# Scan phase: the step size by one softplus activation, both halves in succession

## The chip, the cores and the metric

The kernel runs on one core of one Trainium2 chip. The metric is the device time of one execution in microseconds (us), lower is better. Engines: TensorE (PE), VectorE (DVE), ScalarE (ACT), GpSimd (POOL), and SyncE (SP), which issues most of the DMAs. Each works through its own instructions in the order in which they were written, and waits where an instruction needs a semaphore.

## The reference

Sixteen sequences of 512 tokens with 256 channels pass through a selective scan (the mixer) and then, pairwise independent, through two layers of windowed attention and feed-forward (the stack). Only the mixer matters here. For each sequence:

```python
xz = einsum('bld,ed->ble', h, W_in); x_ssm, z = split(xz, 2)      # 512 inner channels each
A = -exp(A_log)                                                   # 512 x 16 states
B_mat, C_mat = x_ssm @ W_B.T, x_ssm @ W_C.T                       # 16 states each
dt = softplus(x_ssm @ W_dt.T + b_dt)                              # the step size, 512 channels
# for each token: h = exp(min(dt * A, 20)) * h + dt * B * x;  y = sum over states of h * C
y = (y + x_ssm * D) * silu(z)
x = x + ga * (y @ W_out.T * sigmoid(output_gate))
```

## The kernel before

`mixer_pass` handles one sequence in about 109 us. Channels lie on the 128 partitions, tokens along the free axis. The 512 inner channels are four chunks `d`; two chunks are a half. The scan is cut into 32 units `q` of 128 channels x 2 states x 512 tokens: units 0 to 15 belong to the first half, 16 to 31 to the second. For one unit

- ScalarE computes the decays, `exp(dt * A)`, two activations (step `decay`, line 701), into one of three SBUF slots or, for ten units, into PSUM;
- TensorE spreads the rows of B over the partitions (step `bcast`, line 576) and VectorE multiplies them by `u = dt * x` in PSUM (step `mul`, line 762). For the ten units 2, 3, 8, 9, 12, 13, 18, 19, 24, 25 a DMA spreads B and GpSimd multiplies (line 832), so these have no `bcast`;
- VectorE scans (step `scan`, line 779);
- GpSimd multiplies by C (step `cmul`, line 839);
- TensorE adds the unit to the sum over states (step `sum`, line 584), after which its state slot, one of six, is free.

A `bcast` of unit q waits for scan q-2, since the two PSUM slots take turns. The gates (`gate`, line 785) need the last sums of their half: gate 2 that of unit 30, gate 3 that of unit 31.

Beside the units of sequence s-1, in the same pass, the products of sequence s are made in two PSUM banks called `work`, one bank for each product, in turn: `xs`, `bc`, `z` (lines 540 to 551). `dt` (`project_dt`, line 553) is the exception: one half takes both banks at once, twelve matmuls, and it has to wait until both have been read. `softplus` (line 670) then turns a half into the step size. Before, this is done in parts on three engines: ScalarE writes `relu(v)`, `exp(-|v|)`, a mask, a square for a series, and `ln(1 + exp(-|v|))`; VectorE (step `step`, `step_size`, line 748) evaluates the series and puts it where the mask says; GpSimd (step `dtadd`, `add_parts`, line 811) adds the two parts (line 815), then makes `u` (line 818) and sets the marks in `dt` that separate the two states of a unit (line 822). The bank release of `dt` hangs on VectorE's `log_chosen`.

The order of all steps is one list written out by hand, `MIXER_ORDER` (line 140). Each engine takes its own steps from it in that order. The list holds three sequences at once: "-" after a step's name moves it one sequence back. Written with ~ for sequence s-1, the stretch around the change reads, engine by engine:

```
TensorE: sum14~ sum15~ dt0 bcast20~ skip1~ bcast21~ sum16~ sum17~ bcast22~ sum18~ bcast23~ sum19~ sum20~ sum21~
         z0 z1 z2 bcast26~ z3 bcast27~ sum22~ dt1 bcast28~ sum23~ bcast29~ sum24~ sum25~ bcast30~ bcast31~
         sum26~ sum27~ sum28~ bcast0 bcast1 sum29~ sum30~ sum31~ skip0 out0~
ScalarE: decay18~ bcmid0 xscopy3 decay19~ decay20~ decay21~ decay22~ soft0 decay23~ decay24~ zcopy0 decay25~
         zcopy1 zcopy2 decay26~ decay27~ zcopy3 decay28~ decay29~ soft1 decay30~ decay31~ decay0 decay1
VectorE: scan17~ gate0~ bclow0 gate1~ scan18~ scan19~ mul20~ mul21~ scan20~ scan21~ mul22~ mul23~ scan22~ step0
         scan23~ scan24~ scan25~ mul26~ mul27~ scan26~ scan27~ mul28~ mul29~ scan28~ scan29~ mul30~ mul31~
         scan30~ scan31~ mul0 mul1 step1 gate2~ scan0 gate3~ scan1 scan2 scan3
GpSimd:  cmul16~ to cmul21~ mul24~ mul25~ cmul22~ cmul23~ cmul24~ dtadd0 cmul25~ to cmul31~ mul2 mul3 cmul0
         cmul1 dtadd1 cmul2
```

In the first pass there is no sequence before, and only the steps without ~ run: they follow one another with nothing beside them. ScalarE's functions come in table sets; a change of set is an instruction of its own (ACT_TABLE_LOAD). In a pass there are two changes, to silu and back to exp and ln (lines 649 and 650).

Of the kernel before, what the change touches and what calls it, by code (L numbers as in the profile page):

```python
# [22 lines left out]
P = 128  # L23
BATCH, SEQ, DIM = 16, 512, 256
# [3 lines left out]
INNER_CHUNKS = D_INNER // P  # L28
# [6 lines left out]
SERIES_ROOT = 3.0 ** 0.5  # L35
# [11 lines left out]
SERIES_BELOW = 0.02  # L47
# [4 lines left out]
EXP_AND_LN = "natural_log_exp_and_others"  # L52
MOD_SHIFT_A, MOD_SCALE_A, MOD_GATE_A, MOD_SHIFT_B, MOD_SCALE_B, MOD_GATE_B = range(6)
# [48 lines left out]
def host_constants():  # L102
# [32 lines left out]
    1: "xload xT xcopy stat norm hT mod up hcut xs xscopy bc bccopy cstore bcup bcrest bcmid bclow dt soft step dtadd"  # L135
# [8 lines left out]
scan-:15 mul-:16 cload:6 scan-:16 bload:9 mul-:17 bcast-:13 bcrest-:0 decay-:22 cmul-:15 mul-:18 soft-:0 scan-:17  # L144
decay-:23 bcast-:14 bcast-:15 mul-:19 cload:7 cload:8 gate-:0 bclow-:0 gate-:1 cmul-:16 cmul-:17 decay-:24 zcopy-:0
cmul-:18 cmul-:19 cmul-:20 decay-:25 sum-:10 zcopy-:1 cstore:0 sum-:11 bc-:0 bcast-:16 scan-:18 zcopy-:2 decay-:26
decay-:27 cload:9 sum-:12 zcopy-:3 decay-:28 bload:12 scan-:19 bcast-:17 cload:10 decay-:29 cmul-:21 sum-:13 mul-:20
mul-:21 soft-:1 scan-:20 xs-:3 sum-:14 bcast-:18 scan-:21 decay-:30 mul-:22 mul-:23 sum-:15 mul-:24 mul-:25 dt-:0
cmul-:22 decay-:31 scan-:22 bcast-:19 bcast-:20 decay:0 step-:0 skip-:1 scan-:23 decay:1 stat:0 cload:11 bcast-:21
# [3 lines left out]
h2store:0 sum-:22 dt-:1 cmul-:30 bcast-:28 scan-:29 sum-:23 bcast-:29 mul-:30 sum-:24 mul-:31 sum-:25 xcopy:0 decay:6  # L153
bcast-:30 scan-:30 bcast-:31 sq2:0 sum-:26 sum-:27 scan-:31 bload+:1 mul:0 sum-:28 decay:7 mul:1 bcast:0 bcast:1
sum-:29 step-:1 dev2:0 cmul-:31 decay:8 bcast:2 gate-:2 scan:0 mul:2 gate-:3 scan:1 xcopy:1 scan:2 scan:3 decay:9
mul:3 mul:4 res:0 sum-:30 mod:0 cmul:0 scan:4 sum-:31 skip:0 decay:10 out:0 bcast:3 res:1 cmul:1 bcast:4 mul:5 out:1
dtadd-:1 sum:0 bcast:5 up:0 cmul:2 scan:5 xT:0 bcast:6 mod:1 cen2:0 decay:11 up:1 cmul:3 cmul:4 mean2:0 decay:12 mul:6
sum:1 cmul:5 mul:7 scan:6 bcast:7 mul:8 scan:7 xn2:0 decay:13 bload+:4 scan:8 xscopy:0 sum:2 decay:14 decay:15
decay:16 xscopy:1 h2:0 scan:9 mul:9 xscopy:2 bcast:8 cmul:6 var2:0 bccopy:0 mul:10 xT:1 hcut:0 mul:11 cmul:7 cmul:8
sum:3 cmul:9 sum:4 hcut:1 scan:10 scan:11 bcast:9 hT:0 decay:17 bcup:0 hT:1  # L160
# [61 lines left out]
def mixer_pass(nc, inp, mod, x1_dram, stack_dram, bc_dram):  # L222


    with ExitStack() as ctx:
        def sb(name, shape, dt=F32):
            return ctx.enter_context(nc.sbuf_tensor("a_" + name, shape, dt))
# [12 lines left out]
        work = ctx.enter_context(nc.psum_tensor("a_work", [P, 2, SEQ], F32))  # L240
# [8 lines left out]
        skip_mat = sb("skip_mat", [P, INNER_CHUNKS, P])  # L249
# [6 lines left out]
        b_dt = sb("b_dt", [P, INNER_CHUNKS])  # L256
        skip_d = sb("skip_d", [P, INNER_CHUNKS])
        ln_eps = sb("ln_eps", [P, 1])
        root, above = sb("root", [P, 1]), sb("above", [P, 1])
        half_cut = sb("half_cut", [P, 2, 1])  # L260
        waiter = sb("waiter", [P, 2])
        xt = sb("xt", [P, TILES, DIM])
        xn = sb("xn", [P, TILES, DIM])
        neg_mean = sb("neg_mean", [P, TILES])
# [43 lines left out]
        abs_done = signal("abs_done", INNER_CHUNKS)  # L308
        exp_done = signal("exp_done", 2)
        series_begun = signal("series_begun", 2)  # L310
        series_done = signal("series_done", 2)
        log_chosen = signal("log_chosen", 2)
        dt_sum = signal("dt_sum", 2)
# [16 lines left out]
        x1_done = signal("x1_done", CHUNKS)  # L330
# [55 lines left out]
        def first_statistics(act):  # L386
# [4 lines left out]
                      root, above, half_cut, skip_mat, signals, sems_cleared, (neg_mean, token_rate), load_first_x, first_statistics)  # L391
# [8 lines left out]
        sp_p = sb("sp_p", [P, 2, SEQ])  # L400
        sp_ln = sb("sp_ln", [P, 2, SEQ])
        sp_mask = sb("sp_mask", [P, 2, SEQ])
# [17 lines left out]
                    "dt": (log_chosen, 1), "out": (x1_done, 1), "mean2": (xc2_done, 1), "var2": (xn2_done, 1)}  # L420
# [187 lines left out]
        def _(act):  # L608
# [61 lines left out]
            def softplus(s, slot, half):  # L670


                wait(act, x1_done, s - 2, CHUNKS)
                for dd in range(2):
                    d = 2 * half + dd
                    wait(act, dt_full, s, d + 1)
                    nc.scalar.activation(dt[slot][:, d, :], work[:, dd, :], ACT.Relu, bias=b_dt[:, d:d + 1])
                    nc.scalar.activation(work[:, dd, :], work[:, dd, :], ACT.Abs, bias=b_dt[:, d:d + 1]).then_inc(abs_done.sem, 1)
                wait(act, abs_done, s, 2 * half + 2)
                nc.scalar.activation(work[:], work[:], ACT.Exp, scale=-1.0).then_inc(exp_done.sem, 1)  # L680
                wait(act, exp_done, s, half + 1)
# [45 lines left out]
        def _(dve):  # L727
# [20 lines left out]
            def step_size(s, slot, half):  # L748

                wait(dve, series_begun, s, half + 1)  # L750
                nc.vector.scalar_tensor_tensor(work[:], sp_p[:], 13.0 / 16, work[:], ALU.add, ALU.mult).then_inc(series_done.sem, 1)
                wait(dve, series_done, s, half + 1)
                nc.vector.memset(waiter[:, half:half + 1], 0.0)
                nc.vector.copy_predicated(sp_ln[:], sp_mask[:].bitcast(I32), work[:]).then_inc(log_chosen.sem, 1)

# [50 lines left out]
            pipeline(dve, {"hcut": cut_h, "bcrest": rest_of_bc, "bclow": lower_bc, "step": step_size, "mul": scan_input, "scan": scan,  # L806
                           "gate": gate, "res": residual, "cen2": centre_tail, "xn2": normalise_tail})

        @block.gpsimd
        def _(pool):  # L810
            def add_parts(s, slot, half):

                pair = slice(2 * half, 2 * half + 2)
                wait(pool, log_chosen, s, half + 1)
                nc.gpsimd.tensor_tensor(dt[slot][:, pair, :], dt[slot][:, pair, :], sp_ln[:], ALU.add).then_inc(dt_sum.sem, 1)
                wait(pool, dt_sum, s, half + 1)
                wait(pool, xs_done, s, INNER_CHUNKS)
                nc.gpsimd.tensor_tensor(u[slot][:, pair, :], dt[slot][:, pair, :], xs[slot][:, pair, :], ALU.mult)\
                    .then_inc(u_done.sem, 1)
                wait(pool, u_done, s, half + 1)  # L820

                nc.gpsimd.tensor_tensor(dt[slot][:, pair, 0:1], half_cut[:], half_cut[:], ALU.add).then_inc(dt_done.sem, 1)

            def scan_input(s, slot, q):
                if q not in by_pool:
                    return
                j, d, dd = unit(q)
                k = q // 2
                wait(pool, u_done, s, d // 2 + 1)
# [12 lines left out]


# [1020 lines left out]
def setup_weights(nc, inp, banks, ident, mean_mat, pick, picks, w_in_t, w_dt_in, w_bc_in, w_out_t, neg_a, b_dt, skip_d, mod, ln_eps,  # L1864
                  root, above, half_cut, skip_mat, signals, cleared, to_zero, load_first_x, first_statistics):


    with ExitStack() as ctx:
# [42 lines left out]
        with nc.Block() as block:  # L1911
# [68 lines left out]
            def _(dve):  # L1980
# [3 lines left out]
                nc.vector.memset(root[:], -SERIES_ROOT / 4)  # L1984
                nc.vector.memset(above[:], SERIES_BELOW)
# [80 lines left out]
```

## Time and profile before

| | |
|---|---|
| runs | median 4442.51 us of 3 (4442.38 to 4449.84) |
| span of the profiled execution | 4447.4 us |
| busy: TensorE | 4082.2 us (92%) |
| busy: VectorE | 3664.9 us (82%) |
| busy: ScalarE | 2681.4 us (60%) |
| busy: GpSimd | 2692.2 us (61%) |
| VectorE, tenths in 40 slices | `4999999999999999667778787777878777787874` |
| GpSimd, tenths in 40 slices | `2999999999999999553433333343433334433332` |
| granted TensorE clock, tenths | `8999999999999999869999999999999999999998` |

The profile is one execution on the chip. The span is cut into 40 slices of 111 us each; a digit is the busy share in tenths, 9 is 90% or more. The mixer is about the first 41% of the span (to 1850 us), the stack is the rest. In a timeline, a row starts with the start of the instruction and its length, and ends with "xN" where N like instructions in a row are merged; in brackets stands how long the engine was idle before it, and what ended that. Instructions of one engine overlap a little, so the cost of one in a full row is the distance to the next start.

### The profile page before, as it was taken

To read this page: it belongs to the slowest core of one execution; us is meant where nothing else is said; L and a number is where in the kernel's file an instruction comes from. 1 tells how busy PE (TensorE), PEld (TensorE's weight loads), DVE (VectorE), ACT (ScalarE), POOL (GpSimd) and SP (SyncE) were. 2 spreads that over 40 slices of the span, in tenths; PEclk is the share of its full clock that TensorE was granted. 3 is DMA by queue.
4 is the path that set the end of the run, shared out by engine and by line. 5 is a ranking of instruction groups with operands and counts; after the bars stand their busy time and mean duration, and the time that the engine had idled before them with its cause. 6 is when DMAs were issued, how large, how long until landed. Compare 5 with 4: busy or idle time off the path is not lost. (4 is left out here: it accounts for less than half of the span.)

```text
span 4447.4 us, 60346 instructions
## 1 busy us (share of the span) xinstructions
PE 4082.2 (92%) x19614; PEld 2634.6 (59%) x19614; DVE 3664.9 (82%) x6079; ACT 2681.4 (60%) x5831; POOL 2692.2 (61%) x1329
## 2 busy tenths in 40 slices
PE   6999999999999998659999999999999999999997
PEld 4444444444444444347777777776767777677775
DVE  4999999999999999667778787777778787777874
ACT  5677777777777776335656555555646555565654
POOL 2999999999999999553433333343433334343332
PEclk8999999999999999869999999999999999999998
DMA  2333333333333333420000000001020100101000
GB/s 84 107 117 114 115 114 119 115 115 119 119 114 114 115 119 111 141 77 29 15 29 15 29 15 29 15 19 58 20 78 20 34 25 25 34 20 39 20 29 24
DMA packets 118502, 295.05 MB, mean 66 GB/s; under 512 B 21208, under 2 KB 43664, under 8 KB 118192
## 3 DMA queue, kind: packets, MB, share of 16 engines
q1 hardware_dynamic: 114544, 290.37, 19.7%
q8 instruction: 160, 2.62, 0.3%
q10 hardware_dynamic: 3648, 0.83, 0.1%
q14 instruction: 150, 1.23, 0.1%
HBM read 248.52 MB, written 42.64 MB: 65 GB/s over the span
## 5 line engine op out<-in xcount | busy, mean ns | idle before, releaser
L839 POOL TENSOR_TENSOR a_state<-a_state,a_c_wide 128x1024 f32<-128x1024 f32 x512 | 1196.8, 2377 | 32.4 <-DVE a_state L779 31.4
L584 PE MATMUL a_y_sum<-a_state,a_ident 128*128 128x512 f32 x2048 | 948.2, 600 | 2.4 <-POOL a_state L839 2.4
L1667 POOL TENSOR_TENSOR b_scores<-b_scores,b_row_rate 128x1024 f32<-128x1024 f32 (+1 forms) x256 | 426.6, 1682 | 731.0 <-DVE b_row_rate L1782 731.0
L779 DVE TENSOR_TENSOR_SCAN a_state<-a_decay,a_slot 128x1024 f32<-128x1024 f32 x352 | 790.7, 2272 | 3.4 <-issue 0.4
L1640 POOL TENSOR_TENSOR b_by_cos<-b_qk,b_rotary 128x1024 f32<-128x1024 f32 x128 | 309.0, 2414 | 604.3 <-DVE b_qk L1717 604.3
L1340 PE MATMUL b_bank<-b_w_qkv,b_hx_part 128*128 128x512 f32 x2304 | 628.7, 413 | 41.0 <-DVE b_qk L1717 18.3
L584 PEld LDWEIGHTS a_y_sum<-a_state,a_ident 128*128 128x128 f32 x2048 | 388.2, 192 | 407.8 <-issue 343.2
L1545 ACT ACTIVATE b_scores<-b_scores,b_row_bias 128x256 f32<-128x256 f32 (+1 forms) x1024 | 478.0, 471 | 204.8 <-DVE b_row_bias L1771 203.2
L701 ACT ACTIVATE a_decay<-a_dt,a_neg_a 128x512 f32<-128x512 f32 x704 | 458.8, 712 | 107.5 <-DVE a_state L779 105.3
L1340 PEld LDWEIGHTS b_bank<-b_w_qkv,b_hx_part 128*128 128x128 f32 x2304 | 421.3, 193 | 161.0 <-issue 44.0
L1451 PE MATMUL b_bank<-b_hn_part,b_w 128*128 128x512 f32 x2112 | 508.5, 398 | 7.3 <-DVE b_hn_part L1689 7.1
L1451 PEld LDWEIGHTS b_bank<-b_hn_part,b_w 128*128 128x128 f32 x2112 | 396.0, 189 | 103.2 <-DVE b_hn_part L1689 9.6
L762 DVE TENSOR_TENSOR a_slot<-a_u,a_slot 128x1024 f32<-128x1024 f32 x352 | 417.7, 1214 | 23.9 <-PE a_slot L576 23.2
L832 POOL TENSOR_TENSOR a_state<-a_u,a_b_wide 128x1024 f32<-128x1024 f32 x160 | 376.0, 2375 | 4.5 <-PE a_y_sum L584 4.1
L701 ACT ACTIVATE a_slot<-a_dt,a_neg_a 128x512 f32<-128x512 f32 x320 | 208.1, 683 | 280.9 <-DVE a_state L779 280.1
L779 DVE TENSOR_TENSOR_SCAN a_state<-a_slot,a_state 128x1024 f32<-128x1024 f32 x160 | 356.7, 2269 | 2.1 <-ACT a_slot L701 1.2
L1674 POOL TENSOR_TENSOR b_h_part<-b_h,b_h_part 128x512 fp32r<-128x512 f32 x160 | 206.4, 1290 | 248.8 <-ACT b_h_part L1606 248.8
L1765 DVE CUSTOM_DVE_ANT_0 b_scores<-b_bank,b_squares 128x256 f32<-128x256 f32 (+1 forms) x1024 | 338.1, 386 | 0.3 <-issue 0.3
L1837 DVE SCALAR_TENSOR_TENSOR b_h<-b_bank,b_b_1a,b_gelu 128x512 f32<-128x512 f32 x192 | 143.6, 749 | 188.0 <-POOL b_h_part L1674 116.7
L1500 ACT ACTIVATE b_qk_rot<-b_bank 128x512 f32<-128x512 f32 x256 | 142.7, 597 | 242.2 <-PE b_bank L1340 241.4
L1472 PE MATMUL b_bank<-b_h_part,b_w 128*128 128x512 f32 x1088 | 285.9, 401 | 0.0
L576 PE MATMUL a_slot<-a_bc_parts,a_picks 96*128 96x512 bf16 x704 | 212.1, 384 | 80.0 <-DVE a_state L779 79.5
(210 smaller groups left out, 7042.4 us busy)
## 6 DMA issues: line engine op xcount, KB each, us to landing
a_c_wide<-bc_rows SPq DMA_DIRECT2D x256, 512.0 KB, 3.7
a_b_wide<-bc_rows SPq DMA_DIRECT2D x80, 512.0 KB, 4.8
b_hx<-stack_rows SPq DMA_DIRECT2D x64, 256.0 KB, 3.8
b_x_res<-stack_rows SPq DMA_DIRECT2D x32, 512.0 KB, 4.0
a_xt<-in_L_attn_x SPq DMA_DIRECT2D x16, 512.0 KB, 6.1
x_rows<-a_x_t SPq DMA_DIRECT2D x16, 512.0 KB, 5.4
stack_rows<-a_h_t SPq DMA_DIRECT2D x16, 512.0 KB, 5.4
stack_rows<-b_xc SPq DMA_DIRECT2D x16, 512.0 KB, 2.9
```

Source lines behind the costliest of these rows:

```text
L584: last = nc.tensor.matmul(y_sum[dd][:], ident[:], state[state_ring.slot[q]][:, i, :], start=False, stop=(j == GROUPS - 1 and i == GROUP - 1))
L701: last = nc.scalar.activation(to[:, i, :], dt[slot][:, d, :], ACT.Exp, scale=neg_a[:, d, n:n + 1])
L762: nc.vector.tensor_tensor(slots[q % 2][:], u[slot][:, d, :].unsqueeze(1).to_broadcast([P, GROUP, SEQ]), slots[q % 2][:], ALU.mult).then_in ...
L779: nc.vector.tensor_tensor_scan(flat(h), flat(factor), flat(term), 0.0, ALU.mult, ALU.add).then_inc(scan_done.sem, 1)
L832: nc.gpsimd.tensor_tensor(state[state_ring.slot[q]][:], u[slot][:, d, :].unsqueeze(1).to_broadcast([P, GROUP, SEQ]), b_wide[b_ring.slot[k] ...
L839: nc.gpsimd.tensor_tensor(h[:], h[:], c_wide[c_ring.slot[q // 2]][:], ALU.mult).then_inc(cmul_done.sem, 1)
L1340: last = nc.tensor.matmul(psum.tile(name)[:], x[:, c, w * P:(w + 1) * P].bitcast(F32R), weights[:, c, cols:cols + INNER].bitcast(F32R), st ...
L1451: last = nc.tensor.matmul(psum.tile(f"{stem}{m}")[:], weights[:, c, at * P:(at + 1) * P].bitcast(F32R), x[:, c, :].bitcast(F32R), start=(n ...
L1545: e = nc.scalar.activation(scores[w % 2][:, h, lo:hi], scores[w % 2][:, h, lo:hi], ACT.Exp, bias=row_bias[:, w, h:h + 1], accum_out=row_su ...
L1640: nc.gpsimd.tensor_tensor(by_head(by_cos), by_head(qk), for_heads(rotary[:, w, 0], DIM_HEAD), ALU.mult)\
L1667: nc.gpsimd.tensor_tensor(probs, probs, row_rate[:, w, at].unsqueeze(2).to_broadcast([P, 4, hi - lo]), ALU.mult)\
L1765: last = nc.vector.tensor_tensor_reduce(out=scores[w % 2][:, head, lo:hi], in0=psum.tile(f"s{w}_{g}_{h}")[:, at + lo:at + hi], in1=mask[:, ...
```

## The change

The step size becomes one activation `Softplus` with the bias, written directly to `dt`, for each of the four chunks. The relu, abs, exp, mask, square and ln activations go, as do VectorE's `step` and GpSimd's first add. A change of table set to `softplus` stands ahead of half 0, and one back to exp and ln behind half 1. In the order, `soft1` moves right behind `soft0` on ScalarE (from behind decay29~ to ahead of decay23~), and `dt1` right behind `dt0` on TensorE (from behind sum22~ to ahead of bcast20~). Both banks of `dt` are now released by ScalarE's `soft_done`. All other steps keep their order.

```diff
@@ softplus @@
                 wait(act, x1_done, s - 2, CHUNKS)
+                if half == 0:
+                    nc.scalar.preload_act_table_set(SOFTPLUS)
                 for dd in range(2):
                     d = 2 * half + dd
                     wait(act, dt_full, s, d + 1)
-                    nc.scalar.activation(dt[slot][:, d, :], work[:, dd, :], ACT.Relu, bias=b_dt[:, d:d + 1])
-                    nc.scalar.activation(work[:, dd, :], work[:, dd, :], ACT.Abs, bias=b_dt[:, d:d + 1]).then_inc(abs_done.sem, 1)
-                wait(act, abs_done, s, 2 * half + 2)
-                nc.scalar.activation(work[:], work[:], ACT.Exp, scale=-1.0).then_inc(exp_done.sem, 1)
-                wait(act, exp_done, s, half + 1)
-                wait(act, log_chosen, s if half else s - 1, half if half else 2)
-                nc.scalar.activation(sp_mask[:], work[:], ACT.Relu, scale=-1.0, bias=above[:])
-                nc.scalar.activation(sp_p[:], work[:], ACT.Square, scale=1.0 / SERIES_ROOT, bias=root[:])
-                wait(act, dt_sum, s if half else s - 1, half if half else 2)
-                nc.scalar.activation(sp_ln[:], work[:], ACT.Ln, bias=1.0).then_inc(series_begun.sem, 1)
+                    last = nc.scalar.activation(dt[slot][:, d, :], work[:, dd, :], ACT.Softplus, bias=b_dt[:, d:d + 1])
+                last.then_inc(soft_done.sem, 1)
+                if half == 1:
+                    nc.scalar.preload_act_table_set(EXP_AND_LN)
@@ release of the banks @@
-                    "dt": (log_chosen, 1), "out": (x1_done, 1), "mean2": (xc2_done, 1), "var2": (xn2_done, 1)}
+                    "dt": (soft_done, 1), "out": (x1_done, 1), "mean2": (xc2_done, 1), "var2": (xn2_done, 1)}
@@ VectorE @@
-            def step_size(s, slot, half):
-
-                wait(dve, series_begun, s, half + 1)
-                nc.vector.scalar_tensor_tensor(work[:], sp_p[:], 13.0 / 16, work[:], ALU.add, ALU.mult).then_inc(series_done.sem, 1)
-                wait(dve, series_done, s, half + 1)
-                nc.vector.memset(waiter[:, half:half + 1], 0.0)
-                nc.vector.copy_predicated(sp_ln[:], sp_mask[:].bitcast(I32), work[:]).then_inc(log_chosen.sem, 1)
@@ GpSimd, add_parts @@
-                wait(pool, log_chosen, s, half + 1)
-                nc.gpsimd.tensor_tensor(dt[slot][:, pair, :], dt[slot][:, pair, :], sp_ln[:], ALU.add).then_inc(dt_sum.sem, 1)
-                wait(pool, dt_sum, s, half + 1)
+                wait(pool, soft_done, s, half + 1)
                 wait(pool, xs_done, s, INNER_CHUNKS)
```

## Rows read from the trace of the kernel before

**Rows 1.** Busy time by stretches: stretch, us, then each engine, PEclk, DMA share, GB/s.
```profile
1382.19:1491.03 108.84, 100.82 (x299) 48.74 (x298) 108.33 (x72) 78.39 (x134) 107.55 (x49) 1.00 0.35 117
```

**Rows 2.** Timeline of VectorE: start us, us, what, [idle before and releaser].
```profile
1354.11 2.33 DVE L762 TENSOR_TENSOR a_slot<-a_u,a_slot 128x1024 f32<-128x1024 f32 x2
1356.35 4.46 DVE L779 TENSOR_TENSOR_SCAN a_state<-a_decay,a_slot 128x1024 f32<-128x1024 f32 x2
...
1365.17 1.20 DVE L751 SCALAR_TENSOR_TENSOR a_work<-a_sp_p,a_work 128x1024 f32<-128x1024 f32 x1
...
1367.63 2.27 DVE L779 TENSOR_TENSOR_SCAN a_state<-a_decay,a_slot 128x1024 f32<-128x1024 f32 x1
...
1374.18 2.33 DVE L762 TENSOR_TENSOR a_slot<-a_u,a_slot 128x1024 f32<-128x1024 f32 x2
...
1382.19 1.23 DVE L762 TENSOR_TENSOR a_slot<-a_u,a_slot 128x1024 f32<-128x1024 f32 x1 [0.19 <-PE a_slot L576]
...
1396.56 1.23 DVE L751 SCALAR_TENSOR_TENSOR a_work<-a_sp_p,a_work 128x1024 f32<-128x1024 f32 x1
...
1399.07 0.68 DVE L785 TENSOR_TENSOR a_u<-a_y_sum,a_sz 128x512 f32<-128x512 f32 x1
```

**Rows 3.** Timeline of TensorE's matmuls in the same sequence.
```profile
1349.24 3.00 PE L535 MATMUL a_work<-a_h_part,a_w_dt_in 128*128 128x512 f32 x12 [0.70 <-DVE a_bc_parts L745]
1352.16 0.59 PE L576 MATMUL a_slot<-a_bc_parts,a_picks 96*128 96x512 bf16 x2
...
1354.34 0.59 PE L576 MATMUL a_slot<-a_bc_parts,a_picks 96*128 96x512 bf16 x2
...
1367.80 4.40 PE L535 MATMUL a_work<-a_h_part,a_w_in_t 128*128 128x512 f32 x18 [1.10 <-DVE a_sp_ln L754]
...
1381.49 0.60 PE L576 MATMUL a_slot<-a_bc_parts,a_picks 96*128 96x512 bf16 x2
...
1394.55 0.59 PE L576 MATMUL a_slot<-a_bc_parts,a_picks 96*128 96x512 bf16 x2 [0.44 <-DVE a_state L779]
1394.98 5.31 PE L584 MATMUL a_y_sum<-a_state,a_ident 128*128 128x512 f32 x12
```

**Rows 4.** Timeline of ScalarE in the same sequence.
```profile
1349.13 3.78 ACT L701 ACTIVATE a_decay<-a_dt,a_neg_a 128x512 f32<-128x512 f32 x6
1352.81 0.67 ACT L677 ACTIVATE a_dt<-a_work,a_b_dt 128x512 f32<-128x512 f32 x1
1353.38 0.64 ACT L678 ACTIVATE a_work<-a_work,a_b_dt 128x512 f32<-128x512 f32 x1
...
1407.39 1.28 ACT L649 ACT_TABLE_LOAD   x1
1408.68 1.91 ACT L649 ACTIVATE a_sz<-a_sz 128x2048 f32<-128x2048 f32 x1
```

**Rows 5.** Timeline of GpSimd in the same sequence.
```profile
1375.51 2.41 POOL L815 TENSOR_TENSOR a_dt<-a_dt,a_sp_ln 128x1024 f32<-128x1024 f32 x1
1377.99 2.39 POOL L818 TENSOR_TENSOR a_u<-a_dt,a_xs 128x1024 f32<-128x1024 f32 x1
```

**Rows 6.** Timelines of TensorE and ScalarE in the first sequence.
```profile
57.66 3.00 PE L535 MATMUL a_work<-a_h_part,a_w_dt_in 128*128 128x512 f32 x12 [2.62 <-DVE a_bc_parts L745]
68.69 7.99 PE L535 MATMUL a_work<-a_h_part,a_w_in_t 128*128 128x512 f32 x24 [8.02 <-DVE a_sp_ln L754]
...
80.30 1.04 PE L576 MATMUL a_slot<-a_bc_parts,a_picks 96*128 96x512 bf16 x4
...
85.72 2.56 ACT L701 ACTIVATE a_decay<-a_dt,a_neg_a 128x512 f32<-128x512 f32 x4
```

**Rows 7.** Clock: a stretch at half clock, VectorE's stall, TensorE after idle time.
```profile
950.60:954.00 3.40, 3.40 (x6) 1.69 (x5) 3.40 (x3) 1.11 (x2) 3.40 (x2) 0.50 0.49 154
...
958.40 2.36 DVE L762 TENSOR_TENSOR a_slot<-a_u,a_slot 128x1024 f32<-128x1024 f32 x2 [1.42 <-PE a_slot L576]
...
1788.80 0.59 PE L576 MATMUL a_slot<-a_bc_parts,a_picks 96*128 96x512 bf16 x2 [3.43 <-DVE a_state L779]
```

More of the change, by code:

```diff
@@ L34 @@
 POOL_LOADS = (1, 4, 6, 9, 12)
-SERIES_ROOT = 3.0 ** 0.5
 DEPTH, HEADS, DIM_HEAD, WINDOW = 2, 8, 64, 128
@@ L46 @@
 LN_EPS = 1e-5
-SERIES_BELOW = 0.02
 CUT_OFF = 1.2e20
@@ L52 @@
 EXP_AND_LN = "natural_log_exp_and_others"
+SOFTPLUS = "softplus"
 MOD_SHIFT_A, MOD_SCALE_A, MOD_GATE_A, MOD_SHIFT_B, MOD_SCALE_B, MOD_GATE_B = range(6)
@@ L134 @@
 MIXER_STEPS = {
-    1: "xload xT xcopy stat norm hT mod up hcut xs xscopy bc bccopy cstore bcup bcrest bcmid bclow dt soft step dtadd"
+    1: "xload xT xcopy stat norm hT mod up hcut xs xscopy bc bccopy cstore bcup bcrest bcmid bclow dt soft dtadd"
        " z zcopy silu",
@@ L143 @@
 cmul-:14 xscopy-:3 cload:4 decay-:19 cload:5 bcast-:12 sum-:9 decay-:20 xs-:1 xs-:2 decay-:21 mul-:15 scan-:14
[L144 to L149, printed above, removed]
+scan-:15 mul-:16 cload:6 scan-:16 bload:9 mul-:17 bcast-:13 bcrest-:0 decay-:22 cmul-:15 mul-:18 soft-:0 soft-:1
+scan-:17 decay-:23 bcast-:14 bcast-:15 mul-:19 cload:7 cload:8 gate-:0 bclow-:0 gate-:1 cmul-:16 cmul-:17 decay-:24
+zcopy-:0 cmul-:18 cmul-:19 cmul-:20 decay-:25 sum-:10 zcopy-:1 cstore:0 sum-:11 bc-:0 bcast-:16 scan-:18 zcopy-:2
+decay-:26 decay-:27 cload:9 sum-:12 zcopy-:3 decay-:28 bload:12 scan-:19 bcast-:17 cload:10 decay-:29 cmul-:21 sum-:13
+mul-:20 mul-:21 scan-:20 xs-:3 sum-:14 bcast-:18 scan-:21 decay-:30 mul-:22 mul-:23 sum-:15 mul-:24 mul-:25 dt-:0
+dt-:1 cmul-:22 decay-:31 scan-:22 bcast-:19 bcast-:20 decay:0 skip-:1 scan-:23 decay:1 stat:0 cload:11 bcast-:21
 scan-:24 sum-:16 sum-:17 cmul-:23 bcast-:22 sum-:18 bcast-:23 decay:2 sum-:19 scan-:25 decay:3 cmul-:24 sum-:20
@@ L152 @@
 cload:12 bcast-:25 z-:2 mul-:29 bcast-:26 z-:3 scan-:28 cmul-:25 cmul-:26 cmul-:27 norm:0 cmul-:28 cmul-:29 bcast-:27
-h2store:0 sum-:22 dt-:1 cmul-:30 bcast-:28 scan-:29 sum-:23 bcast-:29 mul-:30 sum-:24 mul-:31 sum-:25 xcopy:0 decay:6
+h2store:0 sum-:22 cmul-:30 bcast-:28 scan-:29 sum-:23 bcast-:29 mul-:30 sum-:24 mul-:31 sum-:25 xcopy:0 decay:6
 bcast-:30 scan-:30 bcast-:31 sq2:0 sum-:26 sum-:27 scan-:31 bload+:1 mul:0 sum-:28 decay:7 mul:1 bcast:0 bcast:1
[L155 to L160, printed above, removed]
+sum-:29 dev2:0 cmul-:31 decay:8 bcast:2 gate-:2 scan:0 mul:2 gate-:3 scan:1 xcopy:1 scan:2 scan:3 decay:9 mul:3 mul:4
+res:0 sum-:30 mod:0 cmul:0 scan:4 sum-:31 skip:0 decay:10 out:0 bcast:3 res:1 cmul:1 bcast:4 mul:5 out:1 dtadd-:1
+sum:0 bcast:5 up:0 cmul:2 scan:5 xT:0 bcast:6 mod:1 cen2:0 decay:11 up:1 cmul:3 cmul:4 mean2:0 decay:12 mul:6 sum:1
+cmul:5 mul:7 scan:6 bcast:7 mul:8 scan:7 xn2:0 decay:13 bload+:4 scan:8 xscopy:0 sum:2 decay:14 decay:15 decay:16
+xscopy:1 h2:0 scan:9 mul:9 xscopy:2 bcast:8 cmul:6 var2:0 bccopy:0 mul:10 xT:1 hcut:0 mul:11 cmul:7 cmul:8 sum:3
+cmul:9 sum:4 hcut:1 scan:10 scan:11 bcast:9 hT:0 decay:17 bcup:0 hT:1
 """
@@ L258, in mixer_pass @@
         ln_eps = sb("ln_eps", [P, 1])
-        root, above = sb("root", [P, 1]), sb("above", [P, 1])
         half_cut = sb("half_cut", [P, 2, 1])
-        waiter = sb("waiter", [P, 2])
         xt = sb("xt", [P, TILES, DIM])
@@ L307, in mixer_pass @@
         dt_full = signal("dt_full", INNER_CHUNKS)
[L308 to L313, printed above, removed]
+        soft_done = signal("soft_done", 2)
         u_done = signal("u_done", 2)
@@ L390, in mixer_pass @@
         setup_weights(nc, inp, banks_all, ident, mean_mat, pick, picks, w_in_t, w_dt_in, w_bc_in, w_out_t, neg_a, b_dt, skip_d, mod, ln_eps,
-                      root, above, half_cut, skip_mat, signals, sems_cleared, (neg_mean, token_rate), load_first_x, first_statistics)
+                      half_cut, skip_mat, signals, sems_cleared, (neg_mean, token_rate), load_first_x, first_statistics)
         x_t = [sb(f"x_t{i}", [P, CHUNKS, SEQ]) for i in range(2)]
@@ L399, in mixer_pass @@
         u = [sb(f"u{i}", [P, INNER_CHUNKS, SEQ]) for i in range(2)]
-        sp_p = sb("sp_p", [P, 2, SEQ])
-        sp_ln = sb("sp_ln", [P, 2, SEQ])
-        sp_mask = sb("sp_mask", [P, 2, SEQ])
         bc = sb("bc", [2 * STATES, SEQ])
@@ L804, in normalise_tail @@
                     .then_inc(xn2_done.sem, 1)
-            pipeline(dve, {"hcut": cut_h, "bcrest": rest_of_bc, "bclow": lower_bc, "step": step_size, "mul": scan_input, "scan": scan,
+            pipeline(dve, {"hcut": cut_h, "bcrest": rest_of_bc, "bclow": lower_bc, "mul": scan_input, "scan": scan,
                            "gate": gate, "res": residual, "cen2": centre_tail, "xn2": normalise_tail})
@@ L1864, in setup_weights @@
 def setup_weights(nc, inp, banks, ident, mean_mat, pick, picks, w_in_t, w_dt_in, w_bc_in, w_out_t, neg_a, b_dt, skip_d, mod, ln_eps,
-                  root, above, half_cut, skip_mat, signals, cleared, to_zero, load_first_x, first_statistics):
+                  half_cut, skip_mat, signals, cleared, to_zero, load_first_x, first_statistics):
     with ExitStack() as ctx:
@@ L1983, in _ @@
                     nc.vector.memset(x[:], 0.0).then_inc(cleared, 1)
-                nc.vector.memset(root[:], -SERIES_ROOT / 4)
-                nc.vector.memset(above[:], SERIES_BELOW)
                 nc.vector.memset(half_cut[:], CUT_OFF / 2)
```

## The prediction

> **What bounds the kernel now.** I read the page first, for the slices of the span (they stand in the table above): GpSimd and VectorE are full in the slices of the scan phase, the first 17 or so, and the change touches that phase alone. Then I cut out one steady sequence by a landmark that returns every 108.84 us (1382.19 to 1491.03): in it VectorE is busy 108.33 us, GpSimd 107.55, TensorE 100.82, ScalarE 78.39 [rows 1]. VectorE is therefore the bound with nothing to spare, GpSimd is one step behind, TensorE has 8 us of slack, ScalarE 30. In the timeline of VectorE the reader is to look for the idle times in brackets: in an ordinary sequence there is one, 0.19 us before mul29 [rows 2]. So every microsecond that VectorE stands still is paid in full, and every one taken from it is a gain only if nothing makes it wait instead. The engines' own timelines then show who would make it wait: I walk through one sequence (1347 to 1402 us), keep the durations of its rows and move only what the change moves.
>
> **What is removed.** VectorE loses the two `step` visits. Each is read as the distance to the next instruction: 1365.17 to 1367.63, 2.46 us, and 1396.56 to 1399.07, 2.51 us [rows 2]: 4.97 a sequence. GpSimd loses the first add of each `dtadd`, 1375.51 to 1377.99, 2.48 us [rows 5], 4.96 a sequence. ScalarE loses sixteen activations and gains four and two table loads; with 30 us of slack that is worth nothing by itself, only the place of its work matters. Were this all, the period would be 108.84 - 4.97 = 103.9 us and GpSimd (107.55 - 4.96 = 102.6) and TensorE (100.8) would just allow it.
>
> **What is moved: dt1 and soft1.** The product for the second half uses both work banks, so it waits until soft0 has read them. It now stands on TensorE between dt0 and bcast20, the product that VectorE needs for mul20, so bcast20 and everything after it is queued behind that wait. When is soft0 done? ScalarE runs decay20 to 22 from 1349.13 to 1352.91, directly after decay19, which waits on scan17 [rows 4]; the change then adds a table load ahead of the first softplus, 1.28 us as the load before silu [rows 4]: 1354.21. A softplus of 128x512 from PSUM is not in the trace; the nearest rows are the relu and abs of the same shape and bias, 0.57 us from start to start, 0.67 to the end [rows 4]: both are done at 1354.21 + 0.57 + 0.67 = 1355.45. (If one took 0.1 us more or less, 0.2 us would be added or lost.) TensorE finished dt0 at 1352.2 and stands idle for 3.3 us. dt1 starts at 1355.55 and costs what dt0 does, 2.92 us to the next instruction [rows 3]; bcast20 starts at 1358.47. mul29 waited for its bcast and started 0.70 us after it (1381.49 to 1382.19 [rows 2, 3]), so mul20 starts at 1359.17 where it started at 1354.11 [rows 2]: a stall of 5.06 us. bcast21 follows bcast20 by 2.18 us, since skip1 lies between [rows 3]: ready at 1361.35, while mul20 is over at 1360.28: 1.07 us more. scan20 starts at 1362.48 instead of 1356.35, 6.13 us late. Nothing of this can be made up by VectorE, whose order is fixed.
>
> The wait is rigid: dt0 cannot start earlier, since it waits for bclow on VectorE itself (0.70 us idle before it [rows 3]), and soft0 hangs on scan17 through four decays. Both ends are tied to VectorE, so a new steady state doesn't relax them. The second table load, after soft1 (about 1360.6), is covered: decay23, next on ScalarE, needs scan20, which ends at 1364.8.
>
> **What is late next.** After scan20 the walk gives: step0 gone, so mul26 is wanted at 1374.18 + 6.13 - 2.46 = 1377.85. The four z products follow the sums: z0 started 11.45 us after scan20's start with 1.10 us of idle time [rows 2, 3], now 10.3 after it, 1372.7; bcast26 comes behind z0 to z2, 4.40 us [rows 3], 1377.1, ready at 1377.8: just in time. z3 and bcast27 take some 1.6 + 0.6 us more, 1379.6, and mul27 is wanted at 1378.95: 0.7 us of stall. dt1 no longer stands before bcast28, so the 0.19 us before mul29 go. At mul0 VectorE is then 6.13 - 2.46 + 0.70 - 0.19 = 4.18 us late. On GpSimd cmul20 waits longer for scan20, and what follows is at most 6.1 us late: u0 at 1381.6 instead of the add at 1375.51 [rows 5], 2.6 us for it and the small instruction, then cmul25 to 28 at 2.38 us each (the mean of line 839 on the page), 1393.7. sum28 is wanted at about 1396, so neither it nor bcast0 behind it makes VectorE wait.
>
> At the end of the sequence the second `step` was a cover. gate2 needs sum30. The path is scan31, bcast1, sum29, sum30: bcast1 at 1394.55 + 4.16 = 1398.7, then 0.43 and two sums of 1.72 us [rows 3] and the signal, 1402.75. Without step1, gate2 is wanted at 1396.56 + 4.18 = 1400.74. So 2.0 of the 2.51 us come back as a wait.
>
> Sum for one sequence: 5.06 + 1.07 - 2.46 + 0.70 - 0.19 - 2.51 + 2.0 = +3.7 us. Fifteen sequences overlap with the one before: +56 us.
>
> **The clock.** TensorE's new idle time has a price of its own, bounded by rows. At 950.6 us, behind a stretch with idle times of up to 1.6 us, the granted clock fell from 1.00 to 0.50 (2.4 to 1.2 GHz), and some microseconds later VectorE stood still for 1.42 us at mul0; rows like this last one, 1.2 to 1.5 us, stand in 4 of 15 sequences (first at 193, last at 1505 us) [rows 7]. Against it, an idle time of 3.43 us passed with matmuls at full speed behind it (two in 0.59 us) [rows 7]. The new gap of 3.3 us, and thinner work before bcast28, call for more falls: between 0 and 2 in a sequence at 1.5 us each. I take nearly one more, 1.3 us: the new gap is in length nearest to the row without a fall, but falls came behind much shorter gaps: +20 us, bounds 0 and +45.
>
> **The first sequence.** It has nothing to hide behind: z0 waited 8.02 us for step0 and then dt1, bcast0 and bcast1 came after it; the first decay ran at 85.72 [rows 6]. Now: dt0 over at 60.6, softplus of half 0 done at 61.4, dt1 to 64.4, soft1 to 65.2, z0 to z3 from 65.3 at 5.85 us (four times the 1.46 us that six matmuls of dt0 take) to 71.1, zcopy3 0.6: first decay 71.7. -14 us. The drain of the last sequence has no dt step: 0.
>
> **Total.** 56 + 20 - 14 = +62. Against the profiled span 4447.4: 4509. The span is 4.9 us above the median of the runs (4442.5); on the median, 4504.
>
> **A rule weighed.** The load before silu shows 1.28 us, and the activation starts 0.01 us behind its end [rows 4]. The Trainium skill, "ScalarE: Activation LUTs", section What ACT_TABLE_LOAD costs, adds a drain of about 1.38 us to each switch of sets. By that rule soft0, and with it mul20, would be 1.38 us later and the total 15 x 1.38 = 21 us higher; the trace does not agree, so the sum goes by the row.
>
> **Rivals.**
> Rival 1, on the faster side: bcast20 gets past the waiting dt1. Then the 5.06 + 1.07 us vanish, the rest of the sum stays (-2.4 us a sequence, with few falls of the clock): 4442.5 - 36 - 14 = 4392. It needs TensorE to start a product ahead of one that waits. Against it: in the first sequence bcast0 had its operands from 57.5 us on and free banks, and yet ran at 80.30, behind z0's wait of 8.02 us [rows 6].
> Rival 2, the stalls are smaller: mul20 waits as worked out, but the z products and sum30 are in time (TensorE has slack elsewhere), and the clock doesn't fall. Then 6.13 - 4.97 - 0.19 = +1.0 us a sequence, 15 - 14 = +1: 4443, no change. For it: TensorE's total of 100.8 + 3.3 us is still under the period. Against it: both waits are chains that start at VectorE's own scans.
> Rival 3: every gap brings a fall of the clock that hits dt1 itself, and a second one follows before mul0: 56 + 45 - 14 = +87: 4530.
> Rival 4: a change of table set costs ScalarE more than its load, or a further load appears. Only what lies ahead of soft0 counts; one more load's length there makes 1.28 x 15 = +19 us, 4523. Against it: the silu rows, with nothing between load and activation [rows 4]. (The page named above is the rule for this case.)
>
> **How the numbers follow.** Forecast 0.64, rival 1 0.08, rival 2 (up to -9 and +9 us, and the smaller gains beyond) 0.10, rival 3 0.13, rival 4 0.05. 4504 is the likeliest case. Its own range without a fall of the clock starts at 4484; half of the two small stalls gone as well gives 4464. The top takes in rivals 3 and 4: 4534. Some 0.2% of the time (9 us) is what a measurement tells from no change: faster 0.11, same 0.06, slower 0.83.
>
> **What would show it.** In the trace of the changed kernel: a period near 113 to 114 us by the table loads; 3.3 us idle on TensorE before the second product of w_dt_in, put down to ScalarE's softplus; VectorE idle about 5 us before mul20, 1 before mul21 and 2 before gate2, with GpSimd waiting for scan20; first decay near 72 us; softplus rows of 0.57 us start to start; granted clock under 1.00 in more sequences than four. Wrong is the walk if VectorE is busy without a gap at mul20, or if the period is under 109.

## The result, and the profile after

The changed kernel takes 4529.3 us (median of 4 runs, 4528.1 to 4537.8) against 4446.2 us for the kernel before in the same session (4442.4 to 4450.0). The ratio is 1.019, 95% interval 1.018 to 1.021: 83 us slower. Forecast was 4504, +62.

The page of the changed kernel, span, busy times and three lines of the 40 slices:

```profile
span 4527.4 us, 60006 instructions
...
PE 4126.1 (91%) x19614; PEld 2660.5 (59%) x19614; DVE 3589.5 (79%) x5981; ACT 2566.2 (57%) x5671; POOL 2616.4 (58%) x1297
...
DVE  5999888888888888848777878787867777787874
...
POOL 3988888888888888834343333333333434333332
PEclk8999999999999999969999999999999999999998
```

In the scan phase most of VectorE's and GpSimd's slices are eights where they were nines: both have less to do and stand idle more. In the scan phase the granted clock of TensorE is a nine behind the first slice and doesn't show at this coarseness what follows.

One steady sequence, cut out by the same landmark in two successive sequences (mul20 starts at 1648.47 and at 1764.53), and two short stretches in or near it. Columns as in [rows 1]:

```profile
1648.47:1764.53 116.06, 104.96 (x299) 51.15 (x298) 103.85 (x67) 71.20 (x124) 102.87 (x46) 0.96 0.33 110
1643.00:1647.00 4.00, 4.00 (x10) 3.08 (x10) 0.00 (x0) 0.69 (x1) 2.83 (x2) 0.50 0.22 71
1682.70:1685.50 2.80, 2.80 (x5) 1.22 (x4) 2.80 (x3) 0.02 (x1) 2.00 (x1) 0.50 0.06 23
```

The period (the time from one sequence's mul20 to the next one's) is 116.06 us where it was 108.84. VectorE is busy 103.85 us in it (108.33 before, [rows 1]), so its idle time rose from 0.51 to 12.21 us: 11.70 us of new waits less 4.48 us of removed work are the 7.22 us that the period grew by. The two short stretches show TensorE at half clock (0.50 granted), once under dt1 and once before mul0. Where VectorE stands idle is in its timeline (the rows of before are [rows 2]):

```profile
1648.47 1.23 DVE L739 TENSOR_TENSOR a_slot<-a_u,a_slot 128x1024 f32<-128x1024 f32 x1 [7.69 <-PE a_slot L565]
1650.62 1.23 DVE L739 TENSOR_TENSOR a_slot<-a_u,a_slot 128x1024 f32<-128x1024 f32 x1 [0.92 <-PE a_slot L565]
1651.76 4.46 DVE L756 TENSOR_TENSOR_SCAN a_state<-a_decay,a_slot 128x1024 f32<-128x1024 f32 x2
...
1665.42 2.29 DVE L756 TENSOR_TENSOR_SCAN a_state<-a_slot,a_state 128x1024 f32<-128x1024 f32 x1 [0.40 <-ACT a_slot L686]
...
1689.07 2.36 DVE L739 TENSOR_TENSOR a_slot<-a_u,a_slot 128x1024 f32<-128x1024 f32 x2 [1.51 <-PE a_slot L565]
1692.87 0.69 DVE L762 TENSOR_TENSOR a_u<-a_y_sum,a_sz 128x512 f32<-128x512 f32 x1 [1.44 <-PE a_y_sum L573]
```

In this order: 7.69 us before mul20, 0.92 before mul21, 0.40 before scan25, 1.51 before mul0, 1.44 before gate2. TensorE in the same sequence ([rows 3] before):

```profile
1635.83 3.03 PE L524 MATMUL a_work<-a_h_part,a_w_dt_in 128*128 128x512 f32 x12 [0.69 <-DVE a_bc_parts L730]
1642.22 5.46 PE L524 MATMUL a_work<-a_h_part,a_w_dt_in 128*128 128x512 f32 x12 [3.36 <-ACT a_dt L668]
1647.48 0.89 PE L565 MATMUL a_slot<-a_bc_parts,a_picks 96*128 96x512 bf16 x2
...
1649.92 0.60 PE L565 MATMUL a_slot<-a_bc_parts,a_picks 96*128 96x512 bf16 x2
...
1661.55 4.75 PE L524 MATMUL a_work<-a_h_part,a_w_in_t 128*128 128x512 f32 x18
...
1681.52 7.01 PE L573 MATMUL a_y_sum<-a_state,a_ident 128*128 128x512 f32 x12
```

dt1, the second row, waits 3.36 us for ScalarE and is then 5.46 us long (5.26 to the next instruction), where dt0 in the first row, at the full clock, is 3.03 us long. bcast20 behind it starts at 1647.48 and VectorE's mul20 0.99 us later. ScalarE ([rows 4] before):

```profile
1635.72 3.77 ACT L686 ACTIVATE a_decay<-a_dt,a_neg_a 128x512 f32<-128x512 f32 x6
1639.51 1.28 ACT L664 ACT_TABLE_LOAD   x1
1640.81 1.26 ACT L668 ACTIVATE a_dt<-a_work,a_b_dt 128x512 f32<-128x512 f32 x2
1645.21 0.69 ACT L668 ACTIVATE a_dt<-a_work,a_b_dt 128x512 f32<-128x512 f32 x1 [3.14 <-PE a_work L524]
1647.71 0.69 ACT L668 ACTIVATE a_dt<-a_work,a_b_dt 128x512 f32<-128x512 f32 x1 [1.81 <-PE a_work L524]
1648.42 1.28 ACT L671 ACT_TABLE_LOAD   x1
1654.14 1.33 ACT L686 ACTIVATE a_decay<-a_dt,a_neg_a 128x512 f32<-128x512 f32 x2 [4.43 <-DVE a_state L756]
```

The table load follows the decays with 0.02 us between them, the two softplus are done 2.56 us after its start, and the second load is over 4.4 us before the next decay is allowed to start. GpSimd waits for scan20 here:

```profile
1654.19 4.67 POOL L814 TENSOR_TENSOR a_state<-a_state,a_c_wide 128x1024 f32<-128x1024 f32 x2 [8.36 <-DVE a_state L756]
```

All waits of VectorE between 100 and 1850 us, by who ended them: total us, times, longest. Of the 146.7 us, 112.3 are before mul20 (6.6 to 8.0 us in each of 15 sequences), 20.9 before mul0 (14 times) and 13.4 before mul21.

```profile
DVE a_slot L739 <- PE a_slot L565: 146.7, 44, 8.0
DVE a_u L762 <- PE a_y_sum L573: 22.1, 15, 2.0
DVE a_state L756 <- ACT a_slot L686: 5.8, 15, 0.4
DVE a_state L756 <- POOL a_state L807: 0.5, 2, 0.3
```

Last comes the first sequence, TensorE and then ScalarE's first decay ([rows 6] before):

```profile
58.61 3.04 PE L524 MATMUL a_work<-a_h_part,a_w_dt_in 128*128 128x512 f32 x12 [2.59 <-DVE a_bc_parts L730]
62.52 3.04 PE L524 MATMUL a_work<-a_h_part,a_w_dt_in 128*128 128x512 f32 x12 [0.87 <-ACT a_dt L668]
66.34 5.86 PE L524 MATMUL a_work<-a_h_part,a_w_in_t 128*128 128x512 f32 x24 [0.78 <-ACT a_dt L668]
...
72.73 2.55 ACT L686 ACTIVATE a_decay<-a_dt,a_neg_a 128x512 f32<-128x512 f32 x4
```

### The profile page after: what moved, and what is told of

It is laid out like the page before. It is cut to its first block and busy times, and to the rows that moved or that the text cites. A ratio compares the mean times of both kernels' runs of the same rounds, so it can differ in the third digit from the quotient of the medians.

```text
span 4527.4 us, 60006 instructions
## 1 busy us (share of the span) xinstructions
PE 4126.1 (91%) x19614; PEld 2660.5 (59%) x19614; DVE 3589.5 (79%) x5981; ACT 2566.2 (57%) x5671; POOL 2616.4 (58%) x1297
## 5 line engine op out<-in xcount | busy, mean ns | idle before, releaser
L573 PE MATMUL a_y_sum<-a_state,a_ident 128*128 128x512 f32 x2048 | 964.0, 609 | 0.8 <-POOL a_state L814 0.7
```

What stands on the lines that cost most here:

```text
L573: last = nc.tensor.matmul(y_sum[dd][:], ident[:], state[state_ring.slot[q]][:, i, :], start=False, stop=(j == GROUPS - 1 and i == GROUP - 1))
```

## The experiments

Theory: the order is at fault, dt1 and its wait stand ahead of bcast20, and the idle time that this leaves on TensorE makes its clock fall; the softplus itself is a gain. Rival A: the table loads or the softplus on ScalarE cost the time. Rival B: dt1 is slow for another reason than the idle time. Rival C: there is no room on TensorE for two halves in succession wherever they stand.

### Both halves in their old places

```diff
-... mul-:18 soft-:0 soft-:1 scan-:17 ... mul-:21 scan-:20 ... dt-:0 dt-:1 cmul-:22 ... sum-:22 cmul-:30 ...
+... mul-:18 soft-:0 scan-:17 ... mul-:21 soft-:1 scan-:20 ... dt-:0 cmul-:22 ... sum-:22 dt-:1 cmul-:30 ...
-                if half == 0:
-                    nc.scalar.preload_act_table_set(SOFTPLUS)
+                nc.scalar.preload_act_table_set(SOFTPLUS)
-                if half == 1:
-                    nc.scalar.preload_act_table_set(EXP_AND_LN)
+                nc.scalar.preload_act_table_set(EXP_AND_LN)
```

> The changed kernel with dt1 and soft1 back in their old places; so each half has its own pair of table loads (four a sequence for the step size instead of two). Theory (the order costs the time, the softplus itself gains): no wait at mul20, the 4.97 us of the two steps are gone, against them some 2.0 us before gate2 and 1.4 us before mul27 and mul29: about -1.6 us a sequence, and the shorter first sequence: 4395 to 4425 us. Rival A (the loss comes from the table loads or from softplus on ScalarE): four loads instead of two make it no faster than the changed kernel, 4529 us or more.

Measured: 4400.8 us, ratio to before 0.990 (0.988 to 0.991), the shorter first sequence included. VectorE's waits in one sequence, and its windows row:

```profile
1437.05 2.29 DVE L754 TENSOR_TENSOR_SCAN a_state<-a_slot,a_state 128x1024 f32<-128x1024 f32 x1 [0.40 <-ACT a_slot L684]
...
1447.44 1.23 DVE L737 TENSOR_TENSOR a_slot<-a_u,a_slot 128x1024 f32<-128x1024 f32 x1 [0.37 <-PE a_slot L565]
...
1463.87 0.69 DVE L760 TENSOR_TENSOR a_u<-a_y_sum,a_sz 128x512 f32<-128x512 f32 x1 [1.96 <-PE a_y_sum L573]
...
1447.44:1554.05 106.61, 100.40 (x299) 48.73 (x298) 103.64 (x67) 73.68 (x126) 102.89 (x47) 1.00 0.38 119
```

There is no wait at mul20. What is left are 0.40 us before scan25, 0.37 before mul29 and 1.96 before gate2, the wait for sum30 that step1 used to cover. The period is 106.6 us in most sequences and 107.7 to 108.1 in about every third, which has a fall of the clock and 1.51 us of wait before mul0. Rival A fails as it was put: this kernel has twice as many table loads and is 128 us faster than the changed one.

### The idle time filled

```diff
+FILL = 14
...
                 wait(pe, h_cut, s, CHUNKS)
+                if half and (not isinstance(s, int) or s > 0):
+                    slot_free(pe, s - 1, 20)
+                    for _ in range(FILL):
+                        nc.tensor.matmul(slots[0][:, 0, :], picks[0:96, GROUP * 2, :], bc_parts[1 - slot][0:96, :], start=True, stop=True)
                 banks.wait_free(pe, s, f"dt{half}")
```

> The changed kernel with 14 extra matmuls (bf16, 512 columns, 0.22 us each, 3.0 us in all) between dt0 and dt1, into the PSUM slot that bcast20 overwrites afterwards; their result is used by nobody. Theory (the idle time of 3.36 us makes the clock fall, and this lengthens dt1 by 2.3 us and the signal after it by 0.3): dt1 takes 2.9 us again, the stall at mul20 is 5.1 instead of 7.7 us, the total 15 x 2.6 = 39 us lower, 4485 to 4495; lower still, to 4470, if the fall before mul0 goes too. Rival B (dt1 is slow for another reason, such as the operands or the DMA traffic): 4529 or higher, dt1 still 5.3 us.

Measured: 4496.7 us, 32.5 us less than the changed kernel, with 14 matmuls more in a sequence. TensorE, then VectorE's mul20:

```profile
1384.08 3.18 PE L548 MATMUL a_slot<-a_bc_parts,a_picks 96*128 96x512 bf16 x14
1387.46 3.06 PE L525 MATMUL a_work<-a_h_part,a_w_dt_in 128*128 128x512 f32 x12 [0.20 <-ACT a_dt L673]
1390.36 0.61 PE L570 MATMUL a_slot<-a_bc_parts,a_picks 96*128 96x512 bf16 x2
...
1391.43 1.23 DVE L744 TENSOR_TENSOR a_slot<-a_u,a_slot 128x1024 f32<-128x1024 f32 x1 [5.32 <-PE a_slot L570]
```

The filler ends 0.20 us before dt1, which takes 2.90 us to the next instruction, 3.06 to 3.07 us in length in all 15 sequences with a granted clock of 1.00 under it, and mul20 waits 5.32 us here and 4.96 to 4.98 in the other 14, as the walk without the clock had it (5.06). Rival B fails. The total fell by 32.5 rather than 39 us. Summed over the sequences, the waits before mul20 are 37.4 us shorter (112.3 to 74.9; not 39, since the first three had not had the full fall in the changed kernel, see below). The waits before mul0 are 8.5 us shorter, being there in nine sequences instead of 14. Against that, the waits before gate2 are 2.6 us longer, and ten waits of 0.9 to 1.4 us before mul29, 12.1 us in all, are new. That makes 31 us, as do the two profiled spans (4527.4 and 4496.0 us).

### No table loads, same order

This kernel also leaves out the softplus: relu stands in its place, so its step size is not the reference's.

```diff
-                if half == 0:
-                    nc.scalar.preload_act_table_set(SOFTPLUS)
-                    last = nc.scalar.activation(dt[slot][:, d, :], work[:, dd, :], ACT.Softplus, bias=b_dt[:, d:d + 1])
+                    last = nc.scalar.activation(dt[slot][:, d, :], work[:, dd, :], ACT.Relu, bias=b_dt[:, d:d + 1])
-                if half == 1:
-                    nc.scalar.preload_act_table_set(EXP_AND_LN)
```

> The changed kernel with relu in place of softplus and without the two table loads around it; relu is in every table set, so the step size is not the reference's, all else stays. Theory: soft0 is done 1.28 us earlier, TensorE's idle time before dt1 falls from 3.4 to 2.1 us, the stall at mul20 by 1.3 us with the clock low and by 3.9 if the clock no longer falls there: between 4529 - 19 = 4510 and 4529 - 58 = 4471 us. Rival A (the table loads are the loss): back at the kernel before less its gain, under 4440.

Measured: 4476.3 us, 53 us less than the changed kernel. dt1 on TensorE, and mul20 on VectorE:

```profile
1369.98 3.04 PE L524 MATMUL a_work<-a_h_part,a_w_dt_in 128*128 128x512 f32 x12 [1.93 <-ACT a_dt L666]
...
1373.93 1.23 DVE L735 TENSOR_TENSOR a_slot<-a_u,a_slot 128x1024 f32<-128x1024 f32 x1 [3.95 <-PE a_slot L565]
```

The idle time before dt1 is 1.93 us, 1.43 less; the load's 1.28 us are nearly all of that. Of the 53 us, 15 x 1.28 = 19 are the load on the chain, the other 34 the clock: dt1 took 3.04 us in ten sequences (granted clock 1.00 under it) and 4.6 in five (0.63). So a load on the chain costs its length, and here it also tipped the clock: in this order the loads carry 53 of the 83 us of loss. Without any load the order still loses, by 0.6% (0.5 to 0.8) against the kernel before. The forecast price of the load by itself is confirmed. The loads are not the cause by themselves, as the kernel with four of them in the old places shows, but only where one stands on the chain to dt1.

### dt1 behind bcast21

```diff
-... mul-:25 dt-:0 dt-:1 cmul-:22 ... bcast-:21 scan-:24 ...
+... mul-:25 dt-:0 cmul-:22 ... bcast-:21 dt-:1 scan-:24 ...
```

> The changed kernel with dt1 three steps later, behind bcast21: softplus, both loads and soft1's place as changed. Theory: mul20 and mul21 no longer wait (-6.1 us and the clock's 2.6), in their place some 1.8 us before scan21 (sum16 is late), 1.0 before mul23, 0.7 before mul27, 2.0 before gate2: +0.5 us a sequence against the kernel before, less 13 for the first sequence: 4430 to 4460 us. Rival A: 4529, as softplus and loads are all there. Rival C (two halves in succession cost the same wherever they stand, since TensorE has no room): over 4500.

Measured: 4448.1 us (10 runs), ratio to before 1.000 (0.999 to 1.001): the loss against the kernel before is gone by moving one product past three steps of TensorE. This is the smallest edit of all, and it names the place: dt1 and its wait ahead of bcast20. VectorE's waits in one sequence:

```profile
1465.17 2.29 DVE L756 TENSOR_TENSOR_SCAN a_state<-a_decay,a_slot 128x1024 f32<-128x1024 f32 x1 [1.88 <-PE a_y_sum L573]
...
1469.44 1.23 DVE L739 TENSOR_TENSOR a_slot<-a_u,a_slot 128x1024 f32<-128x1024 f32 x1 [0.86 <-PE a_slot L565]
...
1477.81 2.29 DVE L756 TENSOR_TENSOR_SCAN a_state<-a_slot,a_state 128x1024 f32<-128x1024 f32 x1 [0.59 <-ACT a_slot L686]
...
1504.16 0.69 DVE L762 TENSOR_TENSOR a_u<-a_y_sum,a_sz 128x512 f32<-128x512 f32 x1 [1.96 <-PE a_y_sum L573]
```

1.88 us before scan21 (expected 1.8), 0.86 before mul23 (1.0), 0.59 before scan25, 1.96 before gate2 (2.0); the 0.7 us expected before mul27 did not come. dt1 waits 0.70 us and is 3.02 to 3.04 us long in all 15 sequences. Rival C fails as it was put (over 4500). But two halves in succession, which is what saves one of two pairs of table loads, still cost 47 us more than each half in its old place with two pairs. The waits before scan21 and mul23, which the old places don't have, add up to 28.2 + 13.3 = 41.5 us of that.

### Old places, no table loads

The kernel of the first experiment with relu and without its four loads; the edit is that of the third experiment.

> dt1 and soft1 in their old places, relu in place of softplus and none of the four table loads (the step size is not the reference's, all else stays). Theory: in the old places ScalarE's loads lie beside other work (some 27 us of slack a sequence), so nothing changes against the old places with softplus and loads, 4401 us, but for the first sequence: 4390 to 4403 us. Rival A (a load costs its 1.28 us wherever it stands): 4 x 1.28 x 16 = 82 us less, 4320 us.

Measured: 4397.5 us against 4400.8: the four loads, 82 us of ScalarE's time in all, are worth 3.3 us, within the spread of the runs. The first decay came at 69.92 instead of 72.30 us; 0.95 us of that is dt0 of the first sequence, which started earlier in this execution, and 1.43 us lies behind it.

### The gates later, and more

The base of this edit is the kernel of the first experiment.

```diff
-... dev2:0 cmul-:31 decay:8 bcast:2 gate-:2 scan:0 mul:2 gate-:3 scan:1 ...
+... dev2:0 cmul-:31 decay:8 bcast:2 scan:0 gate-:2 mul:2 scan:1 gate-:3 ...
```

> Old places with softplus and loads, and gate2 and gate3 one step later in the order (gate2 behind scan0, gate3 behind scan1). Theory: the wait of 1.96 us before gate2 is that for sum30, uncovered since step1 went; scan0 covers it again. 26 us less at most, 4375; out0 and the bcasts behind it start no earlier, so up to 1 us of it may come back before mul4: 4375 to 4392 us. Rival: the wait only moves on to mul4 and mul5, 4401 us.

Measured: 4401.4 us, nothing gained against 4400.8. VectorE's waits, and a windows row of a period's length:

```profile
1366.20 1.23 DVE L737 TENSOR_TENSOR a_slot<-a_u,a_slot 128x1024 f32<-128x1024 f32 x1 [0.78 <-PE a_slot L565]
...
1371.78 1.23 DVE L737 TENSOR_TENSOR a_slot<-a_u,a_slot 128x1024 f32<-128x1024 f32 x1 [0.87 <-PE a_slot L565]
...
1300.00:1407.00 107.00, 100.97 (x302) 49.38 (x302) 104.34 (x67) 73.88 (x126) 103.33 (x47) 1.00 0.36 119
```

The 1.96 us before gate2 are gone, and 0.78 before mul4 and 0.87 before mul5 stand in their place, where TensorE has its two products out0 and out1 (3.4 us each) ahead of bcast4 and bcast5. The rival was right. TensorE is busy 100.97 of 107.00 us.

Two more kernels moved more. With bcast0 ahead of sum28 as well:

> The kernel with the gates later and bcast0 ahead of sum28, without the move of zcopy0: between the kernel with the gates later and 15 us under it, 4360 to 4385 us.

Measured 4397.0 us (4394.0 to 4400.6), ratio 0.989 (0.987 to 0.990), not the 4360 to 4385 expected. In the sequences with a fall the wait of 1.5 us before mul0 is gone, and one of 0.82 us before mul1 stands in its place (five sequences). And with zcopy0 behind decay25 too:

> The kernel with the gates later, and two more moves: bcast0 ahead of sum28, so that TensorE's half clock no longer reaches mul0 (up to 1.5 us where it falls), and zcopy0 behind decay25 (0.40 us before scan25). 4355 to 4385 us; it may lose 0 to 10 us if z2 now waits for zcopy0.

Measured 4401.3 us, against 4355 to 4385 expected: the 0.40 us before scan25 are gone, but VectorE, now 0.5 us earlier at mul26, waits 0.55 us for bcast27 at mul27. z0 to z2 ahead of it took 4.92 us instead of 4.75: z2 waits for zcopy0, which ended 0.05 us before z2 started. The four kernels with softplus from 4397 to 4401 us cannot be told apart; the one to keep is the simplest, softplus with both halves in their old places.

## Why the prediction was right, and where it was off

- **VectorE is the bound, and what is taken from it is only a gain if no wait follows.** Right: its idle time rose by 11.70 us a sequence, its busy time fell by 4.48.
- **dt1 stands before bcast20 and waits for soft0.** Right in mechanism and size: 3.3 us of idle time forecast, 3.36 measured; the chain decays, load, two softplus, dt1 is as worked out (softplus 0.57 us start to start, 0.69 long against the 0.67 taken). The 5.06 us of stall at mul20 are what the filler kernel shows (4.97, once 5.32); 1.07 at mul21 was 0.92.
- **The clock.** Here the size was off, by more than the whole miss of 21 us. The sum took 1.3 us a sequence, within bounds of 0 to about 3. In a steady sequence it cost 7.69 - 4.97 = 2.7 us under dt1 (the filler kernel has the 4.97), and the fall before mul0 another 1.51, of which 0.5 came off the wait at gate2 (1.44 for 1.96): 3.7 us, above the upper bound. Over the fifteen sequences of the profile these are 37 + 14 = 51 us where the sum had 20. The step that failed is the choice between the two rows: the idle time of 3.43 us without a fall was taken as nearest. The one before dt1 is as long and has full work on both sides, and the clock fell for it in all 15 sequences: dt1 took 4.3 to 4.6 us in the first three (granted clock 0.63 to 0.66 over its length) and 5.46 in each of the twelve from 482 us on (0.50). A row that shows one escape says little of how often there is none. It was rival 3, every gap brings a fall that hits dt1 and a second follows before mul0, that held. Its total of 4530 against 4529 measured is in part luck: it priced the clock at 45 us instead of 51, counted 10 us of wait at mul27 that did not come, and left out two terms of 5 to 6 us each, the falls before mul0 that the kernel before has already (four, 5.5 us in all) and the wait at scan25. The forecast itself left the same two terms out.
- **mul27.** Wrong, 0.7 us forecast and none measured: z0 came 9.8 us after scan20's start, not 10.3. In its place scan25 waited 0.40 us for decay25, which stands behind zcopy0; the walk had passed over that.
- **gate2.** Right: 2.0 us forecast, 1.96 wherever the clock didn't fall before it.
- **First sequence.** Right: -14 forecast; the first decay came at 72.73 instead of 85.72, -13.0, and dt0 had started 0.95 us later than before, so -14 is right from there on.
- **The sum.** It would be 15 x 7.2 - 13 = 95 us if every sequence were steady. But of the changed kernel's periods the first two were shorter (113.8 and 114.9 us, not yet with the full fall), and four of the kernel before were longer (110.4 to 110.6, each with a fall of the clock before mul0). The profiled spans differ by 80 us, the medians by 83.
- **The rule on table loads.** The drain that the Trainium skill ("ScalarE: Activation LUTs", What ACT_TABLE_LOAD costs) adds to each change of sets doesn't show: the load to softplus starts 0.02 us behind the last decay, and the first softplus 0.02 us behind the load. The measurement decides.
- **Rivals 1, 2 and 4.** bcast20 did not pass the waiting dt1 (1). The wait for sum30 and the clock were not hidden, only the small stall at mul27 was (2). There were two loads a sequence for the step size, and no more (4).

## What to carry to other kernels

Fewer instructions on the engine that is the bound are a gain only as far as the next product or sum is there when it is wanted: walk the chain of the moved step once through the timelines and ask what is queued behind its wait. Saving a change of table sets is not worth an order that puts a wait in front of the busiest engine's input: here it cost 47 us at the better place and 128 at the worse one. Off such a chain, on an engine with slack, the loads were nearly free, 3 us for 64 of them. And removed work may have been the cover of another wait: the second `step` was, for sum30, so that taking out its 2.5 us gained 0.5. Where TensorE has to stand idle ahead of a product that the bound engine waits for, count its clock in: the filler kernel, with 14 useless matmuls in the gap, was 32 us faster than the one without.

## What was not expected of the hardware

The falls of the clock settled into a pattern that repeats with the loop. From the fourth overlapping sequence on, mul20 came 116.0 to 116.2 us after the last in nine of eleven cases (116.4 and then 115.7 around the one at 1416.72), with the clock falling at the same two places each time, while the kernel before had the fall before mul0 in 4 of 15 sequences only. In the kernel of the first experiment the falls before mul0 came from 704 us on every third sequence, 320.8 to 320.9 us apart. With the idle time before dt1 cut to 1.93 us the clock fell there in 5 of 15; with 0.70 us (dt1 behind bcast21) or 0.20 us (filler) in none. Whether the exact repetition is forced by the clock, or only kept up by it, no run here tells.
